# Edge-softmax GNN layer with a mixture-of-experts FFN: a plain addition of the sums, and ScalarE's selections in pairs

## The reference, cut to what matters

```python
q, k, v = xn @ Wq + bq, xn @ Wk + bk, xn @ Wv + bv          # xn = layernorm(x)
e   = edge_attr @ We                                         # one row for each edge
kj  = k[src] + e
alpha = einsum('ehc,ehc->eh', q[dst], kj) / sqrt(C)
ea  = exp(alpha - segment_max(alpha, dst)[dst])
alpha = ea / (segment_sum(ea, dst)[dst] + 1e-16)
out = segment_sum((v[src] + e) * alpha[:, :, None], dst)     # the sums of this case
x   = x + out + (xn @ Ws + bs)
x   = x + FFN(layernorm(x))                                  # gate, top 2 of 8, relu(x W1 + b1) W2 + b2
```

## Time and profile before

| | |
|---|---|
| median of 3 runs | 2572.81 us |
| the profiled execution | 2570.37 us, span 2568.6 us |
| TensorE busy | 2382.9 us (93%) |
| VectorE busy | 2037.0 us (79%) |
| GpSimd busy | 1811.8 us (71%) |
| ScalarE busy | 1577.5 us (61%) |
| granted TensorE clock, mean | 0.964 |

### The profile page before, as it was taken

The page is one execution under the profiler, slowest core; times in us unless marked ns, Lnnn a source line. Parts: engine busy times, 40 slices in busy tenths (PEclk is TensorE's granted clock), DMA queues, the critical chain, the costliest instruction groups (busy, mean ns, idle before and its releaser), DMA issues. The chain is left out here.

```text
span 2568.6 us, 67072 instructions
## 1 busy us (share of the span) xinstructions
PE 2382.9 (93%) x13310; PEld 1992.2 (78%) x13311; DVE 2037.0 (79%) x5261; ACT 1577.5 (61%) x4373; POOL 1811.8 (71%) x2136
## 2 busy tenths in 40 slices
PE   6998999999999999999999999999995657999998
PEld 2445788888888888888888888888883646999998
DVE  6865899999999999999999999999997773222222
ACT  1222677777777677777767777767774224666665
POOL 4123788888888888888888888888886104666666
PEclk9999999999999999999999999999998557999999
DMA  7326777777777777777777777777772753433443
GB/s 229 128 107 187 231 227 221 227 228 228 223 227 227 220 230 224 221 227 226 227 221 226 227 225 229 227 218 220 228 223 78 227 162 60 71 63 64 70 66 55
DMA packets 337693, 476.68 MB, mean 186 GB/s; under 512 B 61318, under 2 KB 268492, under 8 KB 337052
## 3 DMA queue, kind: packets, MB, share of 16 engines
q0 software_dynamic: 92576, 259.72, 37.8%
q1 hardware_dynamic: 238492, 213.23, 28.0%
q10 hardware_dynamic: 6288, 0.05, 0.1%
HBM read 425.40 MB, written 50.57 MB: 185 GB/s over the span
## 5 line engine op out<-in xcount | busy, mean ns | idle before, releaser
L809 POOL DMA_INDIRECT kv_ring<-vk_table,tab_c x880 | 860.6, 978 | 284.3 <-issue 208.2
L963 PE MATMUL ps_e<-we_sb,aT 128*128 128x256 f32 x3520 | 919.5, 384 | 27.9 <-DVE ve_ke L1050 21.6
L963 PEld LDWEIGHTS ps_e<-we_sb,aT 128*128 128x128 f32 x3520 | 601.0, 191 | 102.8 <-issue 48.6
L1044 DVE TENSOR_TENSOR ve_ke<-kv_ring,ps_e 128x512 f32<-128x512 f32 x880 | 599.9, 682 | 38.1 <-PE ps_e L967 24.0
L1014 PE MATMUL ps_u<-ve_ke,sel 128*128 128x264 f32 x1760 | 547.7, 393 | 20.3 <-DVE node_slots L1114 6.8
L819 POOL TENSOR_TENSOR ve_ke<-ve_ke 128x256 f32<-128x256 f32 x880 | 553.4, 633 | 18.5 <-ACT factor L936 4.9
L967 PE MATMUL ps_e<-q_slots,selT 128*128 x1760 | 517.6, 375 | 0.0
L896 ACT COPY aT<-ps_t 128x256 f32<-128x256 f32 x880 | 325.5, 370 | 310.1 <-PE ps_t L951 189.6
L1114 DVE SCALAR_TENSOR_TENSOR node_slots<-node_slots,same_tile,ps_u 128x264 f32 x880 | 423.0, 481 | 29.5 <-DVE node_slots L1099 10.6
L967 PEld LDWEIGHTS ps_e<-q_slots,selT 128*128 128x128 f32 x1760 | 335.1, 190 | 45.9
L1032 DVE TENSOR_REDUCE alpha<-ve_ke 128x8 f32<-128x256 f32 x880 | 365.3, 415 | 5.6 <-issue 3.6
(11 more groups left out here) (249 smaller groups left out, 2642.3 us busy)
## 6 DMA issues: line engine op xcount, KB each, us to landing
a_ring<-in_edge_attr SPq DMA_DIRECT2D x880, 128.0 KB
loc_c<-loc_table SPq DMA_DIRECT2D x220, 128.0 KB
kv_ring<-vk_table,tab_c POOLq DMA_INDIRECT x880
vk_table<-kv_out SPq DMA_DIRECT2D x49, 256.0 KB
skip_table<-skip_out SPq DMA_DIRECT2D x49, 128.0 KB
skip<-skip_table SPq DMA_DIRECT2D x7, 896.0 KB, 10.8
xn_table<-node_slots SPq DMA_DIRECT2D x7, 896.0 KB, 6.5
out<-node_slots SPq DMA_DIRECT2D x1, 6144.0 KB
```

The costliest lines, as they stand in the source:

```text
L809: g.indirect_dma_start(out=kv_ring[:, i % N_KV, :], out_offset=None, in_=vk_table, in_offset=bass.IndirectOffsetOnAxis(ap=tab_c[:, c % N_T ...
L963: t.matmul(ps_e[i % 2][:, 0:D], aT[i % 2][:, k * P:(k + 1) * P], we_sb[:, k, :], start=(k == 0), stop=(k == KD - 1))
L1044: v.tensor_tensor(ve_ke[:, to:ke + 1:ke - to, 0:D], kv.rearrange("p (t d) -> p t d", t=2), e[:, None, :].to_broadcast([P, 2, D]), ALU.add) ...
```

## The change

Two independent edits.

The add. Each item gets a second number, `item_sums_from`: the slot from which the sums so far are read. It is the item's own node tile where the tile goes on, and a slot of zeros behind all others (`ZEROS`) where a new one begins. L1114 then needs no factor and becomes an addition of two tensors. The zero slot is cleared once in the setup, and the row of numbers is worked out there; `same_tile` itself moves into the setup's memory. The node slots and the query slots get 264 columns more. `block_expert` moves into a row of the same tile.

The selections. ScalarE makes two at a time: two L874 into the halves of one buffer, then one L878 over both. The ring `sel` has eight places.

```diff
-N_W = 4
+N_SEL = 8
+        item_sums_from = item_rows[64:65, :]
+            q_words = sb("q_words", [P, (NT + 2) * SLOT + UW], F32R, first_use)
+        sums_flat = sb("node_words", [P, (NT + 2) * SLOT + UW])
+        ZEROS = NT + 2
+                g.memset(sums_flat[:, ZEROS * SLOT:], 0.0).then_inc(first_cleared, 1)
...
                 def masks(step):
                     if step == 0:
                         dve.wait_ge(turned_copied, IB)
+                        v.memset(same_tile[:, 0:1], 0.0)
+                        v.tensor_tensor(same_tile[:, 1:IT], node_tile_rep[:, 1:IT], node_tile_rep[:, 0:IT - 1], ALU.is_equal)
...
                     elif step == 2:
                         v.tensor_tensor(mask, m_lo, m_hi, ALU.add).then_inc(tables_ready, 1)
+                        dve.wait_ge(tables_ready, MASK)
+                        then(v.scalar_tensor_tensor(out=t_rep[:, :], in0=node_tile_rep[:, :], scalar=-float(ZEROS), in1=same_tile[:, :],
+                                                    op0=ALU.add, op1=ALU.mult))
+                        v.tensor_scalar(item_sums_from, t_rep[64:65, :], float(ZEROS), None, ALU.add)
...
                 def select(c, i):
+                    if i % 2:
+                        return
                     m = c * CH + i
...
-                    act.wait_ge(s["summed"], at("summed", m - N_W))
+                    if m >= 4:
+                        act.wait_ge(s["sel_ready"], m - 2)
+                        act.sem_inc(s["act_pace"], 1)
+                    for k in range(2):
+                        nc.scalar.activation(apart[i // 2 % 2][:, k, :], iota_free[:, :], ACT.Abs, scale=-1.0,
+                                             bias=tab_c[:, c % N_TAB, 1, i + k:i + k + 1]).then_inc(s["apart_ready"], 1)
+                    if m >= N_SEL:
+                        act.wait_ge(s["summed"], at("summed", m + 1 - N_SEL))
+                        act.sem_inc(s["act_pace"], 1)
+                    act.wait_ge(s["apart_ready"], at("apart_ready", m + 1))
                     act.sem_inc(s["act_pace"], 1)
-                    nc.scalar.activation(apart[i % 2][:, :], iota_free[:, :], ACT.Abs, scale=-1.0,
-                                         bias=tab_c[:, c % N_TAB, 1, i:i + 1]).then_inc(s["apart_ready"], 1)
-                    act.wait_ge(s["apart_ready"], at("apart_ready", m))
-                    act.sem_inc(s["act_pace"], 1)
-                    nc.scalar.activation(sel[:, i % N_W, :], apart[i % 2][:, :], ACT.Relu, scale=-1.0,
-                                         bias=1.0).then_inc(s["sel_ready"], 1)
+                    nc.scalar.activation(sel[:, m % N_SEL:m % N_SEL + 2, :], apart[i // 2 % 2][:, :, :], ACT.Relu, scale=-1.0,
+                                         bias=1.0).then_inc(s["sel_ready"], 2)
...
+                def sums_from(c, i):
+                    return dve.value_load(item_sums_from[0:1, bass.ds(c * CH + i, 1)], min_val=0, max_val=ZEROS)
+
-                def add(c, i, n, before):
+                def add(c, i, n):
                     m = c * CH + i
-                    to, sofar = [sums_flat[:, bass.ds(k * SLOT, UW)] for k in (n, before)]
+                    to, sofar = [sums_flat[:, bass.ds(k * SLOT, UW)] for k in n]
                     dve.wait_ge(s["summed"], at("summed", m))
                     dve.wait_ge(s["acc_added"], at("acc_added", m - 1))
-                    v.scalar_tensor_tensor(out=to, in0=sofar, scalar=same_tile[:, m:m + 1], in1=ps_u[i % 2][:, 0:UW], op0=ALU.mult, op1=ALU.add
-                                           ).then_inc(s["acc_added"], 1)
+                    v.tensor_tensor(to, sofar, ps_u[i % 2][:, 0:UW], ALU.add).then_inc(s["acc_added"], 1)
...
-                            tiles.append(node_tile_of(c - b, k))
+                            tiles.append((node_tile_of(c - b, k), sums_from(c - b, k)))
```

More of the change, by code:

```diff
@@ L103, in gnn_ffn @@
         put_i = sb("put_i", [P, NB], I32)
-        block_expert_rows = sb("block_expert_rows", [1, NB], I32)
-        block_expert = block_expert_rows[0:1, :]
+        block_expert = item_rows[96:97, 0:NB]
         with ExitStack() as first_use:
-            q_slots = sb("q_slots", [P, NT + 2, SLOT], F32R, first_use)
-        node_slots = sb("node_slots", [P, NT + 2, SLOT])
+            q_words = sb("q_words", [P, (NT + 2) * SLOT + UW], F32R, first_use)
+        sums_flat = sb("node_words", [P, (NT + 2) * SLOT + UW])
+        ZEROS = NT + 2
+        q_slots, node_slots = [w[:, 0:(NT + 2) * SLOT].rearrange("p (j w) -> p j w", w=SLOT) for w in (q_words, sums_flat)]
         q_first, q_second = [q_slots[:, 1:NT + 2, k * D:(k + 1) * D] for k in range(2)]
-        q_moving = [q_slots[:, :, :].rearrange("p j w -> p (j w)")[:, SLOT + k * D:] for k in range(2)]
+        q_moving = [q_words[:, SLOT + k * D:(NT + 2) * SLOT] for k in range(2)]
         x_sb = node_slots[:, 1:NT + 1, D:2 * D]
-        sums_flat = node_slots[:, :, :].rearrange("p j w -> p (j w)")
         values, counts = node_slots[:, 0:NT, 0:D], node_slots[:, 0:NT, D:UW]
@@ L123, in gnn_ffn @@
         carried = sb("carried", [P, NCH], F32, c_soft)
-        same_tile = sb("same_tile", [P, IT], F32, c_soft)
         N_TAB = 4
@@ L174, in gnn_ffn @@
             stepped = sb1("stepped", [NT, IT])
+            same_tile = sb1("same_tile", [P, IT])
             node_tile_rep = sb1("node_tile_rep", [P, IT])
@@ L368, in _ @@
                         resets()
-                pool.wait_ge(first_cleared, 1)
+                pool.wait_ge(first_cleared, 2)
             @block.scalar
@@ L505, in _ @@
                 then(v.memset(q_slots[:, NT + 1, 0:2 * D].bitcast(F32), 0.0))
-                v.memset(same_tile[:, 0:1], 0.0)
-                then(v.tensor_tensor(same_tile[:, 1:IT], node_tile_rep[:, 1:IT], node_tile_rep[:, 0:IT - 1], ALU.is_equal))
                 def floats(step):
@@ L682, in gnn_ffn @@
             ve_ke = sb3("ve_ke", [P, 2 * CH + 2, UW])
-            sel = sb3("sel", [P, N_W, P])
+            sel = sb3("sel", [P, N_SEL, P])
             alpha = [sb3(f"alpha{i}", [P, P]) for i in range(2)]
-            apart = [sb3(f"apart{i}", [P, P]) for i in range(2)]
+            apart = [sb3(f"apart{i}", [P, 2, P]) for i in range(2)]
             am = sb3("am", [P, P])
@@ L1013, in emit @@
                             pe.wait_ge(s["acc_added"], at("acc_added", m - 2))
-                            t.matmul(ps_u[i % 2][:, 0:UW], sel[:, i % N_W, :], ve_ke[:, (par + back) % 2 * CH + i, :],
+                            t.matmul(ps_u[i % 2][:, 0:UW], sel[:, m % N_SEL, :], ve_ke[:, (par + back) % 2 * CH + i, :],
                                      start=True, stop=True).then_inc(s["summed"], 1)
@@ L1136, in emit @@
                             n = tiles.pop(0)
-                            before = last_tile[0] if last_tile else n
+                            before = last_tile[0] if last_tile else n[0]
                             if i == 0:
                                 rescale(c - back, before)
-                            add(c - back, i, n, before)
-                            last_tile[:] = [n]
+                            add(c - back, i, n)
+                            last_tile[:] = [n[0]]
                 over_chunks(dve, emit, what="add", parts={3: "scan", 4: "scan_back", 6: "own", 7: "least", 8: "shift"})
```

## The result

The changed kernel takes 3135.62 us (median; 3134.03 to 3137.41), the kernel before in the same runs 2573.4: a ratio of 1.2185, 95% interval 1.2164 to 1.2207. The forecast was 2682 with a range to 2725. The sign and the place were right, the size was not: +562 us instead of +109.

What follows compares the result with a forecast made beforehand. TensorE and VectorE, both with floors near 30 us a chunk, were taken to bound the loop by waiting for each other. 2570.4 + 92 (loop) + 17 (drain) = 2679; the median lies 2.4 higher: 2682 us, range 2600 to 2725.

Steps and rivals of the forecast that it cites:

- (b): VectorE's queue: a second value load per item, 0.63 us of sequencer each; hidden at most places, paid at three a chunk.
- The bounds, 0.02 and 0.69: Second load's sequencer price in us: 0.02 if only the check is paid, 0.69 if the address arithmetic doubles.
- It becomes 1.69: VectorE's sequencer work per item rises from 1.04 to 1.69 us, still under TensorE's 1.76.
- (a): L1114 on VectorE becomes a plain addition: 0.06 us less an item, bounds 0 and 0.07.
- the three late points: Behind own, least and rescale in each chunk, L1032 comes 0.33, 0.42 and 0.50 us late, together 1.25 us a chunk.
- Where VectorE is in step with TensorE it costs nothing: In the edge loop, L1050 ends 2.05 us behind L1044, and TensorE needs it only at 2.26: no cost.
- the first rival: The second load is hidden by the sequencer running ahead of waits or by overlapping reads: 2558 us, chance 0.11.
- the drain: Adds behind the loop, where nothing hides the load: 1.44 us apart instead of 0.83, +17 us.
- (c): ScalarE's selections in pairs: one of 256 columns takes 0.42 us, less busy time, effect on the whole 0.
- (d): Setup: one more memset on GpSimd, 0 to 0.3 us, and two more VectorE passes, 0 to 2; taken as 0.
- worse than additive: Late L1050s delay TensorE, then VectorE in turn: 2.4 us a chunk and more, 2722 us, chance 0.22.

Runs made afterwards that it cites:

- before_twice: The kernel before with each item's node tile number read twice on VectorE, the second value unused: 2739.0 us, ratio 1.0664.
- row32: The changed kernel with the two rows of numbers exchanged, the sums' source in partition 32 and SyncE's row numbers in 64: 2761.3 us, ratio 1.0756.
- sel_only: The kernel before with only ScalarE's paired selections and the ring of eight: 2570.5 us, ratio 1.0000.
- add_only: The changed kernel with the old selections, one at a time and a ring of four: 3138.2 us, ratio 1.2203.
- behind_before_twice: The kernel before with its number read twice and both reads moved behind the issue of L1032: 2654.5 us, ratio 1.0324.
- behind_before: The kernel before with its one read an item moved behind the issue of L1032: 2564.8 us, ratio 0.9976.
- alternate: The kernel before, still one read an item, but from copies of the row in partitions 0 and 64 in turn: 2611.0 us, ratio 1.0155.
- alternate_32_64: The kernel before, one read an item from copies in partitions 32 and 64 in turn, SyncE's row in 96: 2605.3 us, ratio 1.0129.
- two_nocheck: The changed kernel with both numbers side by side, read by one load of two words, bounds unchecked: 2554.6 us, ratio 0.9936.
- packed: The changed kernel with both numbers in one word, read once unchecked and parted by register arithmetic: 2578.2 us, ratio 1.0026.
- before_nocheck: The kernel before with its one read an item on VectorE unchecked: 2564.8 us, ratio 0.9967.
- one_load_of_two: The changed kernel with both numbers side by side, read by one load of two words, bounds checked: 2693.9 us, ratio 1.0480.

## Why the prediction was wrong

**The step that failed is (b)**: "A second value load per item on VectorE ... Price in the sequencer 0.63 us each", and with it "two TENSOR_LOADs an item on VectorE's queue at 0.30 each". The bounds, 0.02 and 0.69, were for the new load, as if it left the old one alone. Here two loads from both sides of partition 64 take 1.68 us together, not 1.27, so the price of the second is about 1.05. The cost of the +562, from the runs:

| part | us | from |
|---|---|---|
| a second load from the same side | +170 | before_twice |
| both loads cross the border | +374 | changed kernel less row32 |
| what else differs | +22 | row32 less before_twice |
| pairs, ring of eight | 0 | sel_only, add_only |

The parts come to 566, as each run has its own measurement of the kernel before (2568.6 to 2573.4). The 22 us are a remainder and not a price of the second address or the addition: ordinary items are as long in row32 as in before_twice (1.82 against 1.81 to 1.82), and the difference stands at the rescale, 3.17 against 2.65 us from score to score, where L1112 takes 0.62 us in the median and L1099 0.16.

A clue stood in the earlier trace rows: the load had a maximum of 553 ns beside a median of 304. Asking which of the 880 it was, and what was different for it, was the question to put. It is the queue's first; whether that one is slow for the same reason is not shown, but a load of 0.55 us would have opened the bound upward.

**"It becomes 1.69. That is above VectorE's own 1.59 after (a), and 0.07 under TensorE's 1.76"** failed as well. Even with near loads an item takes 1.81. I added up the sequencer's instructions and left out that L1041 waits for the L1032 that the loads themselves hold back: the price is not 1.69 but loads + 0.42 + 0.16. This turned a cost at three points into one at most places; behind_before_twice takes 85 us of it back. What is left, 2654.5 - 2564.8 = 90 us for a second near load, is near the 109 that I gave it, but by luck: nearly half of it stands at place 4 (2.60 us against 1.98 in behind_before), where the scan takes 0.70 us, and not at the three late points. The Trainium skill ("Perfetto Trace Analysis", Sequencer-only Instruction) says that of such a wait only the execution is in the profile, not the time for which it waits; the 50 ns of L1054, with some 0.2 us of standing ahead of them, agree. L1115, the wait behind the rescale for two results (of L1111 and L1112), does not: its row has 503 ns in the median and ends 0.05 us after L1112 does, so there the waiting for the second result is in the row.

```profile
L1112 DVE TENSOR_TENSOR node_words<-node_words,factor x55: 153/573/577, 287.0 to 2507.5; 128x8 f32 x55
```
```profile
L1115 DVEq EVENT_SEMAPHORE  x55: 83/503/507, 287.1 to 2507.6; - x55
```

**"Where VectorE is in step with TensorE it costs nothing"** was empty here: at 2.26 us an item VectorE hardly ever is in step; it waited for TensorE's L980 at 14 of 880 items. And alternate shows where it fails: at place 4, where L1045 waits for TensorE, the sequencer has no lead and the slower load was paid, 0.21 us.

Right were: that the sequencer stands at a waiting instruction and the loads are not taken in advance (the first rival fell); the drain, for near loads 1.46 against 1.44 us (1.91 with the crossing); L1130 at 0.42 us; (c), a pair's selection at 0.417 against 0.42 and no effect; (d), the first score at 231.9 us instead of 229.5. Of the three late points two came in before_twice, L1032 0.91 us behind L1044 after own (0.93 forecast) and 1.01 after the rescale (1.10). The one behind least did not (0.62 against 1.02), and three came that were not forecast, at places 1, 4 and 11 (0.89, 0.92 and 1.05).

The rival "worse than additive" named 2722 and a chain of late instructions between engines. The closed loop is another mechanism, inside one queue, so it was no hit either.

## What to carry to other kernels

Count the sequencer as an engine of its own: loads of registers, checks of bounds and address arithmetic are in no busy share, and showed here only as idle time with "issue" as the releaser. Before adding a load, follow the queue around one full item and look for a wait on something that was issued behind the load: then the loads and that instruction add up, and turning two lines of issue order can be worth more than the instruction saved. Give an operation that the trace shows once per item a second price for "next to another of its kind", and look at its maximum, not the median alone.

## What the runs showed of the hardware

- A TENSOR_LOAD of one word on VectorE's queue takes 0.30 us when the last one came from the same side of the border at partition 64 and 0.52 when not (row32, alternate, alternate_32_64). The stage behind the loop bears it out: there the engines of the changed kernel and of row32 read the experts' numbers from partition 96. In row32 VectorE comes from partition 32, and has one slow load (the maximum); in the changed kernel it comes from 64 and has none, while TensorE's queue, which comes from 0, has one:

```profile
L1606 DVEq TENSOR_LOAD <-item_rows x112: 299/303/535, 2329.3 to 2750.0; - x112
```
```profile
L1606 DVEq TENSOR_LOAD <-item_rows x112: 299/304/319, 2703.5 to 3124.4; - x112
...
L1606 PEldq TENSOR_LOAD <-item_rows x112: 297/302/483, 2705.8 to 3120.7; - x112
```

- The border holds between two tiles too: in alternate VectorE goes from row 64 to the experts' numbers in a tile of one partition (first load 0.53 us), in two_nocheck from such a tile to row 96 (0.54), and in packed from row 64 to row 96 (0.31).
- A second word in the same load costs the same 0.22 us (0.528 for two). The first load of a queue is the slow one too: 0.55, and 0.77 with two words.
- The check of the bounds costs 0.18 to 0.19 + 0.02 us and the gaps behind them for each number, and is worth 8 us where one number is read (before_nocheck), 139 us where two are (one_load_of_two less two_nocheck).
- Why the border costs 0.22 us stays open, and so does where between 32 and 64 it lies; rows other than 0, 32, 64 and 96 were not tried.
- Some of VectorE's instructions take longer while GpSimd works (the scan 0.78 instead of 0.42 us in alternate). That is read from the traces and not tested.
